# A rotary sum moved from VectorE to GpSimd, and weight staging and loads reordered at the start

## What is computed

```python
def _rope(x, sin, cos):
    xe = x[..., ::2]
    xo = x[..., 1::2]
    re = xe * c - xo * s
    ro = xe * s + xo * c
    return jnp.stack((re, ro), axis=-1).reshape(x.shape)

def _attn(xq, ctx, wq, wkv, wo, bo):
    q = _rope(_heads(xq @ wq), sq, cq)
    k = _rope(_heads(k), sk, ck)
    sim = jnp.einsum('bhnd,bhmd->bhnm', q, k) * DH ** (-0.5)
    o = jnp.einsum('bhnm,bhmd->bhnd', jax.nn.softmax(sim, axis=-1), v)
    return o.transpose(0, 2, 1, 3).reshape(...) @ wo + bo
```

## Time and profile before

| | us |
|---|---|
| median of 3 timed runs | 5847.98 (5836.10 to 5848.56) |
| the profiled execution's own time | 5833.79 |
| span of its trace | 5832.0 |
| PE, DVE, ACT, POOL busy | 5350.8, 4342.4, 3384.2, 2536.5 |
| mean granted TensorE clock | 0.962 of full |

### The profile page before, as it was taken

How to read it: one execution, slowest core, us unless ns; L and a number is a source line. 1 busy time by engine, 2 the same in 40 slices (tenths; PEclk the granted TensorE clock), 3 DMA queues, 4 the chain that set the end, 5 groups by cost and what they waited for, 6 DMA issues and landing times.

```text
span 5832.0 us, 167205 instructions
## 1 busy us (share of the span) xinstructions
PE 5350.8 (92%) x66584; PEld 3092.5 (53%) x66584; DVE 4342.4 (74%) x6682; ACT 3384.2 (58%) x7674; POOL 2536.5 (43%) x2193
## 2 busy tenths in 40 slices
PE   6898999999999999999899999999989999999966
PEld 4554555645556455555555556555554645556442
DVE  5888776667888877576888886767688887767734
ACT  3455666565565566666455566666556556665634
POOL 2643534445344443545355344444434435354420
PEclk8999999999999999999999999999999999999976
DMA  4010010101101000010101101010110100101000
GB/s 106 11 38 19 15 31 12 37 12 37 24 12 49 13 26 18 18 30 12 48 14 28 31 13 35 12 32 16 28 31 14 38 19 15 29 9 38 10 17 6
DMA packets 282360, 145.88 MB, mean 25 GB/s; under 512 B 151517, under 2 KB 266813, under 8 KB 281470
## 3 DMA queue, kind: packets, MB, share of 16 engines
q1 hardware_dynamic: 281598, 135.17, 9.7%
HBM read 112.39 MB, written 3.01 MB: 20 GB/s over the span
## 4 chain that ended last, share of the span: by engine, by line
PE 62%; POOL 13%; DVE 12%; issue 7%; ACT 5%; SPq 1%; DMA 0%; POOLq 0%; DVEq 0%; ACTq 0%
PE ring L1595 44%; PE o_acc L1595 17%; POOL weight_sum L1571 12%; DVE max_part L2454 4%; ACT probs L2092 3%; DVE xn L2210 1%; DVE o_inv L2478 1%; DVE raw L2433 1%; DVE raw_sin L2420 1%; POOL hn_rstd L1551 1%; DVE region L2403 1%; PE ring L1713 0%; ACT region L1941 0%; PE ring L1721 0%; DVE raw L2429 0%
## 5 line engine op out<-in xcount | busy, mean ns | idle before, releaser
L2092 ACT ACTIVATE probs<-ring 128x512 f32<-128x512 f32 (+1 forms) x4096 | 2088.2, 571 | 1233.7 <-PE ring L1595 1213.6
L2454 DVE TENSOR_REDUCE max_part<-ring 128x2 f32<-128x800 f32 (+2 forms) x2304 | 2267.2, 1011 | 670.2 <-PE ring L1595 659.1
L1571 POOL TENSOR_TENSOR weight_sum<-weight_sum,probs 128x512 f32<-128x512 f32 (+1 forms) x1408 | 1813.7, 1288 | 229.2 <-ACT probs L2092 90.1
L1571 POOL TENSOR_TENSOR weight_sum<-probs 128x512 f32<-128x512 f32 x256 | 332.9, 1300 | 2052.1 <-ACT probs L2092 1587.1
L1595 PE MATMUL o_acc<-probs,region 128*64 128x256 f32 (+1 forms) x6656 | 903.2, 392 | 0.4 <-ACT probs L2092 0.2
L1595 PE MATMUL ring<-qop,region 64*128 64x256 f16 x9984 | 781.5, 271 | 23.8 <-DVE max_part L2454 8.8
L1595 PEld LDWEIGHTS ring<-qop,region 64*128 64x128 f16 x9984 | 452.3, 95 | 243.5 <-issue 131.6
L1595 PEld LDWEIGHTS o_acc<-probs,region 128*64 128x64 f32 (+1 forms) x6656 | 414.6, 137 | 278.1 <-issue 131.2
L1595 PE MATMUL ring<-shift_q,shift_k 64*128 64x256 f16 (+1 forms) x3840 | 529.7, 270 | 0.0
L2478 DVE RECIPROCAL o_inv<-ring 128x256 f32<-128x256 f32 x256 | 447.4, 1749 | 81.5 <-PE ring L1595 79.6
L1595 PE MATMUL o_acc<-probs,x_nv 128*32 128x256 f32 x6656 | 481.8, 406 | 23.7 <-ACT probs L2092 22.2
(11 more groups left out here) (191 smaller groups left out, 6780.5 us busy)
## 6 DMA issues: line engine op xcount, KB each, us to landing
stage<-in_wide SPq DMA_DIRECT2D x448, 64.0 KB, 2.0
nk<-x_nk SPq DMA_DIRECT2D x768, 25.0 KB
wo_stage<-in_wide SPq DMA_DIRECT2D x32, 512.0 KB, 4.0
ff_w<-in_ff_w SPq DMA_DIRECT2D x48, 256.0 KB, 3.1
stage<-in_wide SPq DMA_DIRECT2D x64, 128.0 KB, 2.6
v_stage<-in_wide SPq DMA_DIRECT2D x128, 64.0 KB, 1.9
ff_w<-in_ff_w SPq DMA_DIRECT2D x16, 512.0 KB, 3.7
v_stage<-kv_split SPq DMA_DIRECT2D x128, 48.0 KB, 1.8
```

The costliest lines, as they stand in the source:

```text
L1571: pool.tensor_tensor(total, before, probs[0:rows_, (un.chunk + k) % PROBS, :], ALU.add)\
L2092: act.activation(to, src, ACT.Exp, scale=t.scale).then_inc(exp_done.sem, 1)
L2454: dve.tensor_reduce(dst, src, AX.X, ALU.max).then_inc(*release(one))
```

## The change

The sum of the two rotary products is issued by GpSimd instead of VectorE; raw_sin has two slots, chosen as raw's; a sine product waits for the sum two operands back. kv_out of sub-layer 1 lies in probs instead of ctx_t, and the first exponential waits for its eight stores; the wait of the context copies for stores moves from piece 0 to piece 4 and asks for those of sub-layer 7 alone. The 28 transfers of narrow weights move from ahead of the program into it as eight items with due times 6 us apart, and the copies of their biases on VectorE move from the first cross prelude to the first narrow one. The splits' due times become the earliest. All tables of due times and WEIGH get other numbers.

```diff
+NARROW_PARTS = 8
 AFTER = {
-    0: {"load": 3.2022, "stats": 0.748, "ln": 1.0684, "ctx": 0.0},
+    0: {"load": 0.2091, "stats": 1.0598, "ln": 6.1346, "ctx": 2.5828},
...
 PACE = {
-    0: 8.0, 1: 28.0, 6: 6.8016, 7: 26.0, 3: 6.0, 4: 21.0, 9: 7.5379, 10: 20.0122
+    0: 8.0, 1: 27.9997, 6: 6.8114, 7: 25.937, 3: 6.0138, 4: 21.0, 9: 7.5379, 10: 19.9299
...
 LEAD = {
-    0: {"op": -3.4609, "low": 1.4036, "max": 0.038, "shift": -0.8166, "val": 0.1455},
+    0: {"op": -5.0531, "low": 4.515, "max": 0.1024, "shift": -1.3726, "val": -0.9543},
...
 SUM_AFTER = {
-    0: 0.6789, 1: 3.9427, 6: 0.8169, 7: 3.2089
+    0: 0.5296, 1: 3.8919, 6: 0.8703, 7: 3.5235
...
+    for i in range(2):
+        put(-600.0 + i, "fetch", i)
     for i in range(len(SPLITS)):
-        put(2.0 + 6.0 * i, "split", i)
+        put(-590.0 + i, "split", i)
+    for i in range(NARROW_PARTS):
+        put(6.0 + 6.0 * i, "narrow", i)
...
-                self.part("DVE", "rope", (due[0], due[1] - 0.5), ("sin", n, j), 0.03 + w * 0.00142, [pe])
-                self.part("DVE", "rope", due, one, 0.05 + w * 0.00142, [("DVE", ("sin", n, j)), ("DVE", ("job", n, j - 1))])
-            self.part("ACT", "op", due, one, 0.17 + w * 0.00083, [("DVE", one) if t.rope else pe])
+                at = ROPE_OPS.index((n, i))
+                before = ROPE_OPS[at - 2] if at >= 2 else None
+                deps = [("POOL", ("job", before[0], op_job(UNITS[before[0]].t, before[1])))] if before else []
+                self.part("DVE", "rope", (due[0], due[1] - 0.5), ("sin", n, j), 0.03 + w * 0.00142, [pe, *deps])
+                self.part("POOL", "rope", due, one, 0.08 + w * 0.0026, [("DVE", ("sin", n, j)), ("DVE", ("job", n, j - 1))])
+            self.part("ACT", "op", due, one, 0.17 + w * 0.00083, [("POOL", one) if t.rope else pe])
...
+        if g == 0:
+            deps.append(("SP", ("split", len(SPLITS) // 2 - 1)))
...
-        raw_sin = sb("raw_sin", [P, ROPE_COLS])
+        raw_sin = sb("raw_sin", [P, 2, ROPE_COLS])
...
-        kv_out = {1: ctx_t[:, :, :, :].rearrange("p u l k -> p (u l k)")[:, 0:H * 3 * P]
+        kv_out = {1: probs[0:DC, :, :].bitcast(F16).rearrange("p g n -> p (g n)")[:, 0:H * 3 * P]
...
+            def load_narrow(i):
+                if i < 4:
+                    for to, at in ((W_NQ, NQ), (W_NK, NK)):
+                        sp.dma_start(narrow_w[:, i, to, :].rearrange("p (h d) -> p h d", d=8),
+                                     spread[:, i, at:at + 4 * P].rearrange("p (h r) -> p h r", r=32)[:, :, 8:16])\
+                            .then_inc(narrow_in, 16)
...
             def program():
                 for one in ORDER_OF["SP"]:
...
+                    elif one[0] == "narrow":
+                        load_narrow(one[1])
...
+                def add_turned(one):
+
+                    un, j = UNITS[one[1]], one[2]
+                    i = un.t.jobs[j][1]
+                    z, w = raw_slot(un, i), N if i == 0 else un.t.kc[i - 1][1]
+                    for product in latest([("job", un.n, j - 1), one]):
+                        pool.wait_ge(*taken(product))
+                    pool.tensor_tensor(raw[:, z, 0:w], raw[:, z, 0:w], raw_sin[:, z, 0:w], ALU.add).then_inc(rope_step.sem, 1)
...
-                        if j == 0 and u == 0:
-                            act.wait_ge(kv_stored, 16 * len(SPLITS))
+                        if j == 4 and u == 0:
+                            act.wait_ge(kv_stored[1], N_STORED)
...
+                    if g == 0:
+                        act.wait_ge(kv_stored[0], N_STORED)
                     act.wait_ge(scores_full.sem, scores_full.at(n, c + 1))
...
-                        old = rope_before(un, i, 1)
                         if old:
 
                             dve.wait_ge(rope_step.sem, rope_step.at(old[0].n, old[0].t.rank(old[1]) + 1))
-                        dve.tensor_tensor(raw_sin[:, 0:w], v, rope_sin[:, a0:a0 + w], ALU.mult)\
+                        dve.tensor_tensor(raw_sin[:, z, 0:w], v, rope_sin[:, a0:a0 + w], ALU.mult)\
                             .then_inc(*release(made))
                         return
...
-                    for product in latest([("job", n, j - 1), made]):
-                        dve.wait_ge(*taken(product))
-                    dve.tensor_tensor(turned, turned, raw_sin[:, 0:w], ALU.add).then_inc(rope_step.sem, 1)
```

More of the change, by code:

```diff
@@ L545, in __init__ @@
                      "close": self.close, "scale": self.scale, "expand": self.expand,
-                     "split": self.split}[one[0]]
+                     "split": self.split, "fetch": self.fetch, "narrow": self.narrow_weights}[one[0]]
             place((time, i), one)
@@ L575, in pre @@
             first = ("first", s, u, m)
-            on("DVE", 0.8, what=first)
+            if (s, u, sub) == (3, 0, 3):
+                on("DVE", 1.4, ("SP", ("narrow", NARROW_PARTS - 1)), what=first)
+            else:
+                on("DVE", 0.8, what=first)
             on("POOL", 1.0, ("DVE", first))
@@ L592, in pre @@
             on("PE", 0.2 if j % 4 == 3 else 0.6, *deps)
-            written = [("SP", ("split", len(SPLITS) - 1))] if j == 0 and u == 0 else []
+            written = [("SP", ("split", len(SPLITS) - 1))] if j == 4 and u == 0 else []
             on("ACT", (0.3 if j % 4 == 3 else 0.7) * (1 if j < 4 else 2), pe, *written)
@@ L602, in pre @@
         elif kind == "fold":
-            on("PE", 0.6, *([("ACT", here(m - 1))] if j else []))
+            on("PE", 0.6, *([("ACT", here(m - 1))] if j else [("SP", ("narrow", NARROW_PARTS - 1))]))
             on("ACT", 0.8, pe)
@@ L610, in pre @@
                 deps = [] if u else [("DVE", here(m - 1))]
+            elif kind == "keys" and u == 0:
+                deps.append(("SP", ("narrow", NARROW_PARTS - 1)))
             on("PE", 0.55 if kind == "keys" and t.cross else 0.45, *deps)
@@ L825, in split, with fetch, narrow_weights @@
     def split(self, due, one):
-        self.part("ACT", "split", due, one, 0.4, [])
+        self.part("ACT", "split", due, one, 0.4, [("SP", ("fetch", one[1] * 2 // len(SPLITS)))])
         self.part("DVE", "split", due, one, 0.55, [("ACT", one)])
         self.part("SP", "split", due, one, 0.6, [("DVE", one)], 4.0)
+    def fetch(self, due, one):
+        self.part("SP", "split", due, one, 0.6, [], (1.0, 4.0)[one[1]])
+    def narrow_weights(self, due, one):
+        self.part("SP", "narrow", due, one, 3.6 if one[1] < 4 else 1.9, [], 2.5)
     def expand(self, due, one):
@@ L1357, in load_weights @@
                 if un.t.cross and un.u == 0 and un.p == 0:
-                    wait((kv_stored, 16 * len(SPLITS)))
+                    for stored in kv_stored:
+                        wait((stored, N_STORED))
                 for k in range(sets):
@@ L1584, in program @@
                         pre(one)
+                    elif one[0] == "job":
+                        add_turned(one)
                     elif one[0] == "scale":
```

135 lines of the change are left out of this document (69 added, 66 removed).

## The result

The changed kernel takes 5750.64 us in the median (5743.84 to 5759.82, four runs), the kernel before 5842.04 (5834.03 to 5848.56) beside it. The ratio is 0.9846, with a 95% interval of 0.983 to 0.9863: 90 us less, where 47 were forecast. The direction was right and the time lies inside the range of 5747 to 5850, at its low edge, but the gain is nearly twice the forecast. The profiled execution took 5753.32 us, its span 5751.5.

The account below looks back on a forecast made before the run. TensorE, busy 5350.8 of 5832.0 us, was taken as the bound, leaving 481 us idle to win. Terms -22 - 20 - 5 - 4 - 4 + 8 = -47 us, from the median 5847.98, gave 5801 us, range 5747 to 5850.

Parts of the forecast that it names:

- part 3: Refitted due times, reordering all five queues in every stage: taken as 0, with 15 us to either side.
- parts 1 and 2: The earlier start, -22 us, and the rotary sum's move to GpSimd, -20 - 5 - 4 - 4 + 8 us.
- part 2: Moving the 448 sums of two rotary products from VectorE to GpSimd: -20 - 5 - 4 - 4 + 8 us.
- The seven later self stages: Self-attention stages after the first: TensorE idle 21 us in all, of which a fifth is won, -4 us.
- The start, -22: First projection at 37 to 42.5 us instead of 63.58: -22 us, bounds -17 and -27.
- The first cover named: At the start, VectorE is what is late next, with work up to 37.70 us.
- The four terms for the sum: Shared stages -20 us, first cross stage -5, first self-attention stage -4, seven later ones -4.
- the +8: Rotary operands later by 0.5 us plus GpSimd's queue, and weight sums with rotary sums among them: 8 us lost.
- Low halves more blocked, 35 us: VectorE's low halves stand still more behind GpSimd, 135 us for about 100; VectorE's net relief 283 - 35 = 248 us.
- Blocked low halves: Rival, chance 0.19: each low half on VectorE meets a GpSimd operation, 237 us; only the start remains, 5826 us.
- The weight sums become the end: Rival, chance 0.15: in cross units rotary sums delay GpSimd's weight sums and TensorE's column sum, +37 us, 5885.
- All VectorE waits go: Rival, chance 0.14: the second slot and free GpSimd remove TensorE's waits behind VectorE, -99 us, 5749.

Follow-up runs that it names:

- both_old: The changed kernel with the due times and duration factors (WEIGH) of the kernel before: ratio 0.9973 to the kernel before.
- before_jit1: The kernel before with a random amount of up to 0.3 us either way added to each entry of its tables, same work: ratio 1.0145.
- pool_only: The kernel before with only the rotary sum on GpSimd and two slots of sine products, old tables and start: ratio 1.0024.
- start_only: The kernel before with only the change's staging, transfers and waits at the start; sums on VectorE, one used slot, old tables: ratio 0.9944.
- undo_dve: The changed kernel with the rotary sum back on VectorE in planner and code, both slots and new tables kept: ratio 1.0056 to the kernel before.
- fix_first2: The changed kernel, order kept, with the sums of the first two units of each rotary self stage on VectorE: ratio 0.9843 to the kernel before.
- after_tiny: The changed kernel in its own order, with GpSimd's rotary sum over 8 columns only: ratio 0.981 to the kernel before.
- before_tiny: The kernel before in its own order, with VectorE's rotary sum over 8 columns instead of 256 to 401: ratio 0.9901.
- narrow_first: The changed kernel with the 28 narrow transfers issued ahead of the program again, orders kept: ratio 0.9877 to the kernel before.

## Why the prediction was right in direction and wrong in size

**The step that failed is part 3.** The refit was priced at 0 with 15 to either side, for the reason that no row prices an order. The runs do: taking the old tables in the changed kernel costs 74 us (both_old), an unsystematic change of up to 0.3 us costs 85 to 126. The forecast's sum treated the refit as a term beside the others, and it isn't one: without it parts 1 and 2 bring 16 us where the forecast had 47; with it they and the refit bring 90. The 74 us are what it costs to be off the fitted tables, not by themselves what a better order is worth. The bound was large enough here (idle time of TensorE, 481 us less the start, of which 72 went), but it is not the whole of what a rearrangement can move: at the same work TensorE's busy time is 5342.6 us in the changed kernel, 5350.8 in before and 5413.1 in before_jit1, and the clock goes with it (last section).

**A second term failed inside part 2.** The seven later self stages were to give 4 us, a fifth of TensorE's idle time in them. They got 38 us longer with the new tables and 41 with the old (pool_only), and stay as they were where the sums are planned on VectorE (456 in start_only, 460 in undo_dve). The shared stages had -20 and got 25 us shorter with the old tables and 73 with the new. Why the self stages lose is open: with orders kept, the first two units' sums are not it (fix_first2), and shorter sums take only 10 us off (487 in after_tiny).

The 90 us split roughly as follows: the length of the sums 37 (before_tiny, after_tiny, orders kept), the start 18 (narrow_first, transfers alone, order kept) to 33 (start_only, planned anew), and what is left, 20 to 35 us, is the better order together with the second slot and the fixed part of the moved instructions, give or take 15. The last is an inference by difference and not measured by itself, and its low end would still fit part 3's 15 us; that part 3 was mis-sized rests on both_old.

**The start, -22.** Right in its mechanism. Forecast 37 to 42.5 us for the first projection, it is 42.23, the upper case, in which the split and the low halves both stand ahead. The first cover named, VectorE's earlier work, is what is late next: its second split starts at 37.48 against 37.70 forecast. The stores of sub-layer 1 are issued from 32.90, and the first exponential, at 61.03, waits for TensorE and not for them. The stage ends 18.3 us earlier, and narrow_first has 18 for the transfers; that is inside the bounds of 17 and 27, but start and first stage's sums together were to give 26. That GpSimd's normalisation holds up the first sum until 43 to 45 came so (45.16 + 0.34, then the sum at 45.47, whose second product is done at 44.68: 0.8 us lost).

**The sum's mechanics.** 1088 and 1037 ns for 1.06 us forecast at 400 and 401 columns, 419 us in all as forecast, GpSimd 2924.6 for 2955 and VectorE 4100.6 for 4094. VectorE's hit is luck: 283 less 35 were forecast, the 35 didn't come, and its busy time still fell by only 242, as records of instructions that follow each other overlap (37.48 + 2.76 is past the 40.17 of the next), so that the sums' 283 us, added one by one, are more than they take of the engine. The shared stage's waits behind max_part halved (6.7 to 3.2), the terms for the seven shared stages and the first cross stage pointed the right way, and in the latter the waits behind ScalarE's qop went from 10.0 to 1.8. But the 6.7 is the largest of its kind: over all seven shared stages these waits went from 38 us (not 47) to 24, and over the whole span only from 85.3 to 80.9. In the shared stages TensorE's idle time fell by far more, from 106 to 60 us, so that max_part was too narrow a row to price them by. The four terms for the sum and the +8 add up to -25; by the sums' length, with orders held, it was 37.

**Low halves more blocked, 35 us.** Wrong, and without effect on the sum. I scaled their blocked time with GpSimd's share; it didn't grow: 755 ns for 771 at 400 columns, and 322 us for 327 over all 448. The reading of the earlier trace rows was also a little off: the sum ends at 79.59, 0.27 us behind GpSimd's operation, and the free one of 256 columns to compare with takes 0.41 us (at 80.52 in the same trace). The Trainium skill, SBUF — State Buffer, section Who interferes with whom, has it that a VectorE instruction with two SBUF inputs and a GpSimd one that reads SBUF exclude each other. The step from the rule to a price was mine: it needs the two to meet, and how often they do, no busy share says.

**The rivals.** "Blocked low halves" is out by the same row. "The weight sums become the end" is out: the waits behind weight_sum are 1.8 us in the shared stage and fell from 55.7 to 41.1 over the span. "All VectorE waits go" has 5749, nearest to the time, but its mechanism didn't happen: the waits behind max_part stand at 80.9 us. That it comes out at the right number is an accident of size. What was missing is a rival in which the refit gains, or is needed for anything to be gained.

**Open.** What the second slot of raw_sin is worth by itself was not tried. Nor was a fresh refit of the kernel before, so a part of the 20 to 35 us might be had without the change. It is not known either how the fitted numbers work: the fitted orders have fewer places where TensorE waits behind maxima than the disturbed ones (178 and 175 for 212 to 228), but no run separates which of them matter. Whether another refit comes lower than 0.9846 is open too; fix_first2 at 0.9843 is the same within its interval, and no kernel of these beats the changed one.

## What to carry to other kernels

Where a planner writes a fixed order for engines that wait for one another, an edit and its refit are one change: price the work from rows, but don't price the refit at zero, and never judge an edit by a run with tables fitted to the other version. Measure a part by keeping the order and shrinking the operation (8 columns here), or compare disturbed with disturbed; to learn how large the loss from an unfitted order is, disturb the tables at random once or twice before anything else. And carry a term from one stage to its likes only after looking at that wait over the whole span.

## What the runs showed of the hardware

**A short wait of TensorE can cost clock as well as time.** Windows of before_jit1 (columns as in the earlier trace rows; the clock is the third number from the end), from two places:

```profile
1990.00:1995.00 5.00, 5.00 (x48) 2.31 (x44) 3.20 (x6) 2.00 (x6) 4.70 (x4) 1.00 0.00 0
1995.00:2000.00 5.00, 3.39 (x42) 1.34 (x40) 4.06 (x5) 2.83 (x6) 3.96 (x4) 1.00 0.02 3
2000.00:2005.00 5.00, 5.00 (x44) 1.86 (x42) 3.37 (x4) 1.08 (x2) 0.72 (x1) 0.51 0.01 2
2005.00:2010.00 5.00, 4.65 (x40) 1.39 (x36) 2.85 (x4) 2.66 (x6) 0.00 (x0) 0.50 0.00 0
2010.00:2015.00 5.00, 4.47 (x76) 2.48 (x76) 4.78 (x8) 4.45 (x10) 0.00 (x0) 0.97 0.02 3
...
3920.00:3925.00 5.00, 5.00 (x66) 3.11 (x64) 1.99 (x4) 2.40 (x8) 4.63 (x4) 1.00 0.15 39
3925.00:3930.00 5.00, 3.42 (x46) 2.11 (x44) 2.02 (x5) 2.63 (x9) 3.92 (x4) 1.00 0.17 44
3930.00:3935.00 5.00, 5.00 (x54) 3.92 (x49) 2.86 (x5) 2.57 (x7) 1.05 (x2) 1.00 0.15 39
```

At the first place TensorE is idle for 1.6 us of the second window, and in the next ten the granted clock is at 0.5, the 1.2 GHz level, with the engine busy. At the second it is idle for as long, and the clock stays at 1.00. So such a wait may be followed by half clock or not; which of them are, no run here shows.

The mean clocks say what it adds up to. Span times the missing share is 5832.0 x 0.038 = 222 us for before, 5751.5 x 0.037 = 213 for after and 5935.7 x 0.049 = 291 for before_jit1. In these traces the 41 us more of idle time of before_jit1 came with 69 us more of clock. The clock also differs between executions of one kernel (198 to 258 us in the eleven of before that ran beside it), so the medians over all executions are the better figures: 266 us for before_jit1, 228 for before, 38 more. pool_only is the clearest case:

```profile
core 0: 5844.6 us, clock 0.954
```

Its TensorE is idle for 461 us, 20 less than in before, and still it is slower, for it loses 5844.6 x 0.046 = 269 us to the clock, 47 more than before in its trace and 35 more by the medians (257 for 222). The waits of a trace, summed, don't give its time. The last 240 us show it from the other side: 241.4 us in before and 250 to 253 in sixteen of the other nineteen kernels here, the changed one too, with some 16 us more lost to half clock in the changed one and the same idle time (88 us in both).

**More work on GpSimd did not make VectorE's low halves longer.** GpSimd does 388 us more in the changed kernel, and the low halves are no longer than before (755 against 771 ns at 400 columns). With GpSimd as little busy as in before they took more in undo_dve (814 ns, GpSimd 2528.0 us). So GpSimd's busy time doesn't set their length; that the order does is likely, and not shown by itself.
